# A third pair of decay buffers, in SBUF, for the Mamba stage of a four-layer cross-attention network

## The chip, the core and the metric

The kernel runs on one core of one Trainium2 chip. The metric is device time in microseconds (us) of that core. The kernel before takes 6634.21 us, the median of 3 runs (6632.14 to 6638.02).

## What is computed

Eight sequences x (512 x 256) and a short context of 64 x 192 for each pass through four blocks, all in float32: self-attention, cross-attention and feed-forward (L0), four Mamba layers on 64 + 512 positions (L1), cross-attention and feed-forward (L2), and a last cross-attention (L3). The change lies in L1, whose core is a scan over time for each of 512 channels and 16 states:

```
dt = softplus(einsum('bsr,er->bse', dt, dtp_w) + dtp_b)
A = -exp(A_log)
dA = exp(dt[..., None] * A)
dBu = dt[..., None] * Bm[:, :, None, :] * xi[..., None]
def step(h, t):
    da, dbu, c = t
    h = da * h + dbu
    return (h, einsum('bes,bs->be', h, c))
```

`dA` are the decays. The context is used by L0, by the 64 positions that go ahead of L1, and again by L2 and L3.

## The kernel before

The program is eight stages (`STAGES`). In the Mamba stage each of the 4 layers is cut into 9 chunks of `TC` = 512 positions, so there are 36 steps. In a step the 512 channels x 16 states are 64 units of 128 partitions x 512 positions, taken two at a time: 32 pairs, numbered j. Five engines run over the same 32 pairs, each in an order that is written out by hand, held together by semaphores.

- **ACT** (`@block.scalar`) makes the decays of a unit with an exponential (L2474) and writes them into PSUM, `banks[:, slot_of(i), :]`. There are two pairs of such buffers, PSUM banks 0, 1 and 2, 3, used in turn. Before it refills a pair it calls `slots_free` (L2123), which waits until the pair two before is done with it and copies the last column of that scan into `state` (L2129 or L2133), the start of the next step's scan. Between the pairs ACT does the rest of the layer: bias, Silu, Softplus, with loads of its function tables around them, at places given by `E_OUT`, `G_OUT`, `F_OUT`, `H_OUT`, `SILU_AT`.
- **POOL** (`@block.gpsimd`) writes dt * B * x of a pair into a ring of 6 pair buffers in SBUF (L2506), one instruction of 128 x 1024 on two SBUF tensors.
- **DVE** (`@block.vector`) scans each unit (L2429): inputs are the decays and the ring's entry. Of the 32 pairs, 22 are DVE's own: the scan writes over the decays in PSUM, and DVE then multiplies by C into the ring (`times_c`, L2237). The other 10 (`BY_POOL`) are POOL's: the scan writes into the ring, ACT copies the state and raises `kept`, and POOL multiplies by C (L2511). The multiplication of a pair's second half comes behind the next pair's first scan.
- **PE** (`@block.tensor`) sums each pair over the states (L2384), and `summed` gives the ring's place back to POOL. PE also does the layer's projections.
- **SP** (`@block.sync`) moves rows and weights by DMA.

All other tensors of the stage lie in `core.work` and `core.weights`, in SBUF. The PSUM has 8 banks: 0 to 3 hold decays, 4 and 5 sums, 6 and 7 the other results. `core.C` (128 x 2 x 512, SBUF) holds the context. The stage does not use it; `final_norm`, which comes next, reads it (L2558, L2688).

Of the kernel before, what the change touches and what calls it, by code (L numbers as in the profile page):

```python
# [18 lines left out]
ALU = mybir.AluOpType  # L19
ACT = mybir.ActivationFunctionType  # L20
AX = mybir.AxisListType

P = 128
B, T, D, DC = 8, 512, 256, 192
PRE, S1 = 64, 576
KD = D // P
M = 64
# [1704 lines left out]
TC = 512  # L1732
CHUNKS = B * S1 // TC
STEPS = LAYERS * CHUNKS
BODIES = 2 * CHUNKS
UN = 64
PAIRS_N = UN // 2
GROUPS = DI // 64
SP_ = DS // 2
BY_POOL = ((0, 5), (0, 3, 6), (0, 4), (0, 2, 4))  # L1740
NQ = sum(len(a) for a in BY_POOL)
ND = PAIRS_N - NQ
# [129 lines left out]
def val(N, per, off):  # L1872

    l, j = N
    return l * (BODIES * per) + (j * per + off)
# [31 lines left out]
    return BEFORE_S[name] if N[1] == -2 else val(N, len(LANE_S), S_BASE + LANE_S[name])  # L1907


def mamba(core):  # L1910
    at = 0
    ring, at = core.area(at, RING, 2, TC)
    dt_rep, at = core.area(at, 2, 2, TC)
# [7 lines left out]
    state, at = core.area(at, UN)  # L1921
    decay, at = core.area(at, UN)
# [5 lines left out]
    bc = core.weights[0][:, 0:SP_ * 2 * TC].rearrange("p (a c t) -> p a c t", a=SP_, c=2)  # L1928
# [22 lines left out]
    u_done, kept, saved = S("u_done"), S("kept"), S("saved")  # L1951
    rep_in = [S("rep_in0"), S("rep_in1")]
    da_full, fed, scanned, prod_d, prod_q, summed = S("da_full"), S("fed"), S("scanned"), S("prod_d"), S("prod_q"), S("summed")
    gated = S("gated")
    y_full, y_free, y_added = S("y_full"), S("y_free"), S("y_added")

    by_pool = lambda j: j % SP_ in BY_POOL[j // SP_]
    d_index = lambda j: sum(not by_pool(i) for i in range(j))
    q_index = lambda j: sum(by_pool(i) for i in range(j))
    slot_of = lambda i: 2 * (i // 2 % 2) + i % 2  # L1960
    da_full_at = lambda N, i: val(N, UN, i + 1)
    fed_at = lambda N, j: val(N, PAIRS_N, j + 2)
    scanned_at = lambda N, i: val(N, UN, i + 1)
    prod_d_at = lambda N, j: val(N, ND, d_index(j) + 3)
    saved_at = lambda N, j: val(N, ND, d_index(j) + 3)
    prod_q_at = lambda N, j: val(N, NQ, q_index(j) + 1)
    summed_at = lambda N, j: val(N, PAIRS_N, j + RING + 1)
    gated_at = lambda N, k: val(N, KI, k + 3)
# [151 lines left out]
        e.wait_ge(ln.v_full, v_at(N, f"H{tv}"))  # L2120
        e.activation(dt[:, tv, :], lane_v, ACT.Softplus, bias=lv("dt_b", tv)).then_inc(ln.v_free, 1)

    def slots_free(e, N, n, j):  # L2123

        M, j = (N, j - 2) if j >= 2 else (previous(N), PAIRS_N + j - 2)
        m = n if M[1] == N[1] else n - 1
        if N[1] >= 0 and by_pool(j):
            e.wait_ge(scanned, scanned_at(M, 2 * j + 1))
            e.activation(state[:, 2 * j:2 * j + 2], ring_pair(m, j)[:, :, TC - 1], ACT.Copy).then_inc(kept, 1)  # L2129
        elif N[1] >= 0:  # L2130
            s = slot_of(2 * j)
            e.wait_ge(prod_d, prod_d_at(M, j))
            e.activation(state[:, 2 * j:2 * j + 2], banks[:, s:s + 2, TC - 1], ACT.Copy).then_inc(saved, 1)  # L2133
            e.wait_ge(saved, saved_at(M, j))

    RESIDUAL = (19, 18)
# [97 lines left out]
    def times_c(e, N, n, j, h):  # L2234

        i = 2 * j + h
        last = e.tensor_tensor(ring_pair(n, j)[:, h, :], banks[:, slot_of(i), :], bc[:, j % SP_, 1, :], ALU.mult)  # L2237
        if h == 1:
            last.then_inc(prod_d, 1)

# [28 lines left out]
    def spread_u(e, k):  # L2269

        s = k % 2
        for h in range(2):
            for q in range(2):
                e.dma_start(u_rep[64 * q:64 * q + 64, s, h, :], u[64 * h:64 * h + 64, k, :]).then_inc(rep_in[s], 16)
# [6 lines left out]
    def load_bc(e, N, a, q, b):  # L2281

        e.dma_start(bc[64 * q:64 * q + 64, a, :, :], scratch[b][:, 2 * a + q, :].partition_broadcast(64)).then_inc(bc_ready[a // 2], 16)

    with core.nc.Block() as block:
        @block.sync
        def _(e):
            store_bc(e, (0, -1), 0)
            e.wait_ge(bc_stored, 16)
            for a in range(2):  # L2290
                for q in range(2):
                    load_bc(e, (0, -1), a, q, 0)
            e.wait_ge(u_done, u_done_at((0, -1), 0, 2))
            spread_dt(e, 0)
            spread_u(e, 0)
            for a in range(2, SP_):
                for q in range(2):
                    load_bc(e, (0, -1), a, q, 0)
            e.wait_ge(u_done, KI)
            for l in range(LAYERS // 2):  # L2300
                for j in range(BODIES):
                    N, c = (l, j), j % CHUNKS
                    layer = l * 2 + j // CHUNKS
                    after = (l * 2 + 2) % LAYERS if j >= CHUNKS else l * 2 + 1
                    e.wait_ge(summed, summed_at(previous(N), PAIRS_N - 1))
                    spread_dt(e, 1)
                    spread_u(e, 1)
                    if c == CHUNKS - 1:
                        load_z(e, core, after)
                    e.wait_ge(scanned, scanned_at(N, 15))  # L2310
                    spread_dt(e, 2)
                    spread_u(e, 2)
                    if c == CHUNKS - 2:
                        load_first(e, core, after)
                    store_bc(e, N, (j + 1) % 2)
                    e.wait_ge(scanned, scanned_at(N, 31))
                    spread_dt(e, 3)
                    e.wait_ge(bc_stored, val(N, 16, 32))
                    spread_u(e, 3)
                    if c == 0:  # L2320
                        load_out(e, core, layer)
                    e.wait_ge(u_done, u_done_at(N, 0, 2))
                    spread_u(e, 0)
                    e.wait_ge(scanned, scanned_at(N, 47))
                    spread_dt(e, 0)
                    if c == CHUNKS - 2:
                        load_middle(e, core, after)
                    for a in range(SP_):
                        pair = 3 * SP_ + a
                        if by_pool(pair):  # L2330
                            e.wait_ge(prod_q, prod_q_at(N, pair))
                        else:
                            e.wait_ge(prod_d, prod_d_at(N, pair))
                        load_bc(e, N, a, 0, (j + 1) % 2)
                        load_bc(e, N, a, 1, (j + 1) % 2)
            for a in range(SP_ // 2):
                e.wait_ge(bc_ready[a], 64 * (STEPS + 1))
            e.wait_ge(rep_in[0], 128 * (2 * STEPS + 1))
            e.wait_ge(rep_in[1], 128 * 2 * STEPS)
            e.wait_ge(core.first_loaded, FIRST_LOAD * (LAYERS + 1))  # L2340
            e.wait_ge(core.z_loaded, Z_LOAD * (LAYERS + 1))
            e.wait_ge(core.middle_loaded, MIDDLE_LOAD * (LAYERS + 1))
            e.wait_ge(core.out_loaded, OUT_LOAD * (LAYERS + 1))
# [50 lines left out]
        def _(e):  # L2394
# [15 lines left out]
            for l in range(LAYERS // 2):  # L2410
                for n in range(BODIES):
                    N, c = (l, n), n % CHUNKS
                    layer = l * 2 + n // CHUNKS
                    for i in range(UN):
                        j, h = i // 2, i % 2
                        k, a = j // SP_, j % SP_
                        if c == CHUNKS - 2 and i == SCALE_AT:
                            e.wait_ge(core.first_loaded, layer * FIRST_LOAD + 2 * FIRST_LOAD)
                        early_dve(e, N, i, c, normed[:, n % 2])
                        for f in range(KI - 1):  # L2420
                            if i == 16 * (f + 1) + 7:
                                gate(e, N, f, z[:, n % 2])
                        if i == 7:
                            gate(e, previous(N), KI - 1, z[:, (n + 1) % 2])
                        if h == 0:
                            e.wait_ge(fed, fed_at(N, j))
                        e.wait_ge(da_full, da_full_at(N, i))
                        da, ub = banks[:, slot_of(i), :], ring_pair(n, j)[:, h, :]
                        e.tensor_tensor_scan(ub if by_pool(j) else da, da, ub, state[:, i:i + 1], ALU.mult, ALU.add).then_inc(scanned, 1)  # L2429
                        if h == 0 and j > 0 and not by_pool(j - 1):  # L2430
                            e.wait_ge(scanned, scanned_at(N, i - 1))
                            times_c(e, N, n, j - 1, 1)
                        if h == 1 and not by_pool(j):
                            e.wait_ge(scanned, scanned_at(N, i - 1))
                            times_c(e, N, n, j, 0)
                        if h == 1 and j == PAIRS_N - 1 and not by_pool(j):
                            e.wait_ge(scanned, scanned_at(N, i))
                            times_c(e, N, n, j, 1)
# [8 lines left out]
        def _(e):  # L2447
# [9 lines left out]
            for l in range(LAYERS // 2):  # L2457
                for n in range(BODIES):
# [7 lines left out]
                    for i in range(UN):  # L2466
# [2 lines left out]
                        if i % 16 == 0:  # L2469
                            e.wait_ge(rep_in[k % 2], rep_at(N, k))  # L2470
                        if h == 0:
                            slots_free(e, N, n, j)
                        f = (2 * k + h) * SP_ + a
                        e.activation(banks[:, slot_of(i), :], dt_rep[:, k % 2, h, :], ACT.Exp, scale=decay[:, f:f + 1]).then_inc(da_full, 1)  # L2474
                        if c == CHUNKS - 1 and i == H_OUT[0]:
                            e.wait_ge(core.middle_loaded, layer * MIDDLE_LOAD + 2 * MIDDLE_LOAD)
                        if c == CHUNKS - 2 and i == E_OUT[0]:
# [351 lines left out]
```

## Time and profile before

| | before |
|---|---|
| median of 3 runs | 6634.21 us |
| the profiled execution, its time | 6639.8 us |
| the profiled execution, its span | 6638.0 us |
| Mamba stage, first scan to last | about 2054 to 5994 us, 3940 us |
| PE, DVE, POOL, ACT busy over the span | 92%, 74%, 66%, 55% |
| granted TensorE clock over the span | 0.941 of 2.4 GHz |

The profiled execution's time is its span and 1.8 us around it. A row of the lines view gives a line of the code, its engine and operation, what it writes and reads by name (`banks` is PSUM; `work`, `weights`, `C`, `X` are SBUF), the shape, the count, then busy time and mean length, and at the end how long the engine sat idle just before such instructions and for whom. A matmul's busy time has modelled ends, so PE's share is not to be taken for PE at its peak. An instruction's recorded length overlaps the next one's start a little on DVE and POOL.

### The profile page before, as it was taken

How to read it: one execution, taken by the hardware profiler on the slowest of the kernel's cores; microseconds unless marked ns; L12 is line 12 of the kernel's file. 1: busy time of each engine (PE TensorE's matmuls, PEld its weight loads, DVE VectorE, ACT ScalarE, POOL GpSimd, SP SyncE). 2: the span in 40 equal slices, each digit the busy share in tenths (PEclk: the TensorE clock that was granted, in tenths of full speed). 3: DMA queues.
4: the chain of work that ended last, by engine and by line, in shares of the span. 5: the costliest groups of instructions: out<-in, count | busy, mean ns of one | idle time of the engine just before them, and what ended most of it. 6: DMA issues, size and time to landing. Idle time of an engine off the chain costs nothing. (4 is left out here: it accounts for less than half of the span.)

```text
span 6638.0 us, 60681 instructions
## 1 busy us (share of the span) xinstructions
PE 6129.0 (92%) x20586; PEld 2577.4 (39%) x20586; DVE 4928.1 (74%) x5709; ACT 3620.5 (55%) x6605; POOL 4394.1 (66%) x2056
## 2 busy tenths in 40 slices
PE   9999999999999989898899989898989898988898
PEld 4555555544443333323333323333323343323444
DVE  4444445543225999999999999999999999995623
ACT  4444445432225666666666666666666666664432
POOL 3333334323005999999999999999999999992300
PEclk9999999999998989899989999999999898989998
DMA  2000000213002333333333333332333232332000
GB/s 80 1 1 1 1 1 1 86 26 102 20 0 68 83 76 78 78 93 85 72 89 71 83 88 86 71 89 65 89 81 93 65 89 65 93 80 56 4 0 26
DMA packets 228678, 387.64 MB, mean 58 GB/s; under 512 B 46304, under 2 KB 64416, under 8 KB 225936
## 3 DMA queue, kind: packets, MB, share of 16 engines
q1 hardware_dynamic: 228368, 383.75, 23.7%
q8 instruction: 164, 2.69, 0.2%
q14 instruction: 146, 1.20, 0.1%
HBM read 207.14 MB, written 23.40 MB: 35 GB/s over the span
## 5 line engine op out<-in xcount | busy, mean ns | idle before, releaser
L2506 POOL TENSOR_TENSOR work<-work,weights 128x1024 f32<-128x1024 f32 x1152 | 2685.6, 2361 | 15.8 <-PE banks L2384 6.8
L2429 DVE TENSOR_TENSOR_SCAN banks<-banks,work 128x512 f32<-128x512 f32 x1584 | 1985.7, 1272 | 53.5 <-ACT banks L2474 48.1
L2384 PE MATMUL banks<-work 128*64 128x512 f32 x4608 | 1353.9, 670 | 378.2 <-POOL work L2511 271.1
L2474 ACT ACTIVATE banks<-work 128x512 f32<-128x512 f32 x2304 | 1496.0, 680 | 25.5
L1992 PE MATMUL banks<-work,weights 128*128 128x512 f32 (+31 forms) x3796 | 1140.6, 451 | 3.0 <-DVE work L2222 3.0
L2237 DVE TENSOR_TENSOR work<-banks,weights 128x512 f32<-128x512 f32 x1584 | 1056.0, 668 | 0.0
L2511 POOL TENSOR_TENSOR work<-work,weights 128x1024 f32<-128x1024 f32 x360 | 848.0, 2356 | 238.4 <-ACT work L2129 238.4
L2429 DVE TENSOR_TENSOR_SCAN work<-banks,work 128x512 f32<-128x512 f32 x720 | 911.2, 1269 | 99.8 <-ACT banks L2474 97.2
L603 POOL TENSOR_TENSOR work<-work 128x1024 f32<-128x1024 f32 x256 | 479.6, 1893 | 743.4 <-DVE work L470 742.9
L1992 PEld LDWEIGHTS banks<-work,weights 128*128 128x128 f32 x3796 | 634.4, 190 | 600.0 <-issue 523.6
L2133 ACT ACTIVATE work<-banks 128x2 f32<-128x2 f32 x792 | 135.9, 172 | 1227.4 <-DVE work L2237 1225.6
L2384 PEld LDWEIGHTS banks<-work 128*64 128x64 f32 x4608 | 271.0, 145 | 1236.4 <-issue 500.8
L553 ACT ACTIVATE work<-banks,work 128x512 f32<-128x512 f32 x512 | 347.7, 690 | 201.1 <-DVE work L464 201.1
L464 DVE TENSOR_REDUCE work<-banks 128x2 f32<-128x1024 f32 x256 | 308.8, 1214 | 105.1 <-PE banks L389 104.7
L2010 PE MATMUL banks<-work,weights 128*128 128x512 f32 x592 | 350.7, 722 | 0.0
L1040 PE MATMUL banks<-work,weights 128*128 128x512 f32 x768 | 341.5, 599 | 9.4 <-ACT work L215 9.4
L454 DVE COPY work<-banks 128x512 f32<-128x512 f32 x256 | 175.5, 685 | 160.3 <-PE banks L379 160.3
L379 PE MATMUL banks<-ident,work 128*128 128x128 f32 x2048 | 277.9, 279 | 8.2 <-DVE work L454 4.6
L379 PEld LDWEIGHTS banks<-ident,work 128*128 128x128 f32 x2048 | 222.1, 141 | 151.7 <-issue 111.1
L389 PE MATMUL banks<-work 64*128 64x512 f32 x1024 | 254.4, 615 | 0.0
L366 PE MATMUL banks<-work 128*64 128x256 f32 x2048 | 247.5, 385 | 0.0
L322 PE MATMUL banks<-work,weights 128*128 128x512 f32 x512 | 224.9, 597 | 6.4 <-ACT work L215 4.2
(312 smaller groups left out, 6796.9 us busy)
## 6 DMA issues: line engine op xcount, KB each, us to landing
weights<-mamba_bc SPq DMA_DIRECT2D x592, 256.0 KB, 5.0
work<-work SPq DMA_DIRECT2D x1160, 128.0 KB, 2.3
weights<-mamba_taps SPq DMA_DIRECT2D x5, 2048.0 KB, 7.5
weights<-cross_vo SPq DMA_DIRECT2D x16, 512.0 KB, 6.9
mamba_taps<-work SPq DMA_DIRECT2D x4, 2048.0 KB, 7.8
cross_vo<-weights SPq DMA_DIRECT2D x6, 1024.0 KB, 8.4
work<-in_conv_rows SPq DMA_DIRECT2D x16, 256.0 KB, 6.7
out_T<-X SPq DMA_DIRECT2D x8, 512.0 KB, 3.3
```

Source lines behind the costliest of these rows:

```text
L379: mm = e.transpose(core.banks[:, 4 + j, kt * P:(kt + 1) * P], probs[:, 2 * (g % 2) + u, j, kt * P:(kt + 1) * P], core.ident[:])
L553: last = e.activation(probs[:, slot, j, :], core.banks[:, 2 * u + j, :], ACT.Exp, bias=nmax[:, slot, j:j + 1], accum_out=sums[:, slot, j:j ...
L603: e.tensor_tensor(probs[:, slot], probs[:, slot], rsum[:, slot, :].unsqueeze(2).to_broadcast([P, 2, T]), ALU.mult) \
L1040: mm = e.matmul(bank(i), w1[:, k, m * P:(m + 1) * P], normed[:, k, :], start=(k == 0), stop=(k == KD - 1))
L1992: mm = e.matmul(lane[:, a:b], conv_w[j][:, k, m * P:(m + 1) * P], nb[:, k, a + j:b + j], start=(d == 0 and k == 0), stop=(j == 0 and b == ...
L2010: mm = e.matmul(lane, z_w[:, k, m * P:(m + 1) * P], nb[:, k, TAPS - 1:], start=(k == 0), stop=(k == KD - 1))
L2237: last = e.tensor_tensor(ring_pair(n, j)[:, h, :], banks[:, slot_of(i), :], bc[:, j % SP_, 1, :], ALU.mult)
L2384: mm = e.matmul(ybank[k % 2][64 * h:64 * h + 64, :], fold, ring_pair(n, j)[:, h, :], start=False, stop=(a == SP_ - 1))
L2429: e.tensor_tensor_scan(ub if by_pool(j) else da, da, ub, state[:, i:i + 1], ALU.mult, ALU.add).then_inc(scanned, 1)
L2474: e.activation(banks[:, slot_of(i), :], dt_rep[:, k % 2, h, :], ACT.Exp, scale=decay[:, f:f + 1]).then_inc(da_full, 1)
L2506: e.tensor_tensor(ring_pair(n, j), u_rep[:, k % 2], bc[:, a, 0, :].unsqueeze(1).to_broadcast([P, 2, TC]), ALU.mult) \
L2511: e.tensor_tensor(ring_pair(n, q), ring_pair(n, q), bc[:, q % SP_, 1, :].unsqueeze(1).to_broadcast([P, 2, TC]), ALU.mult) \
```

## The change

The decays get a third pair of buffers: `core.C`, the context's place. `decay_slots` gives each of the 36 x 32 pairs the buffer that was used longest ago. In the last step only the two PSUM pairs are used, and SP loads the context back into `core.C` from DRAM there (`reload_context`). `slots_free` now waits for the pair that had the same buffer, mostly three before, and copies the states of all pairs up to it. In `saved_at` (L1965) the offset 3 becomes 1, since the copies are now counted from the first pair on.

```diff
+def decay_slots():
+    slot, earlier, last = [], [], [None, None, None]
+    for g in range(STEPS * PAIRS_N):
+        slots = range(3) if g < (STEPS - 1) * PAIRS_N else range(2)
+        s = min(slots, key=lambda t: -1 if last[t] is None else last[t])
+        slot.append(s)
+        earlier.append(last[s])
+        last[s] = g
+    return slot, earlier
...
-    slot_of = lambda i: 2 * (i // 2 % 2) + i % 2
+    slot, earlier = decay_slots()
+    decays = [banks[:, 0:2, :], banks[:, 2:4, :], core.C[:]]
+    pair_at = lambda N, j: val(N, PAIRS_N, j)
+    decay_pair = lambda N, j: decays[slot[pair_at(N, j)]]
...
-    def slots_free(e, N, n, j):
-        M, j = (N, j - 2) if j >= 2 else (previous(N), PAIRS_N + j - 2)
...
+    def keep_state(e, g):
+        M, j = step_of(g), g % PAIRS_N
+        if by_pool(j):
             e.wait_ge(scanned, scanned_at(M, 2 * j + 1))
+            e.activation(state[:, 2 * j:2 * j + 2], ring_pair(M[1], j)[:, :, TC - 1], ACT.Copy).then_inc(kept, 1)
+        else:
             e.wait_ge(prod_d, prod_d_at(M, j))
+            e.activation(state[:, 2 * j:2 * j + 2], decay_pair(M, j)[:, :, TC - 1], ACT.Copy).then_inc(saved, 1)
+
+    def slots_free(e, N, j):
+        g = earlier[pair_at(N, j)]
+        if g is None:
+            return
+        before = earlier[pair_at(N, j) - 1]
+        for m in range(0 if before is None else before + 1, g + 1):
+            keep_state(e, m)
...
-        last = e.tensor_tensor(ring_pair(n, j)[:, h, :], banks[:, slot_of(i), :], bc[:, j % SP_, 1, :], ALU.mult)
+        last = e.tensor_tensor(ring_pair(n, j)[:, h, :], decay_pair(N, j)[:, h, :], bc[:, j % SP_, 1, :], ALU.mult)
...
+    def reload_context(e):
+        M, j = step_of(last_in_c), last_in_c % PAIRS_N
+        e.wait_ge(saved, saved_at(M, j)) if not by_pool(j) else e.wait_ge(scanned, scanned_at(M, 2 * j + 1))
+        e.dma_start(core.C[:, 0, :], core.dram["ctxT"][0:P]).then_inc(context_back, 16)
+        for r in (0, DC - P):
+            e.dma_start(core.C[r:r + DC - P, 1, :], core.dram["ctxT"][P:DC]).then_inc(context_back, 16)
...
-                        da, ub = banks[:, slot_of(i), :], ring_pair(n, j)[:, h, :]
+                        da, ub = decay_pair(N, j)[:, h, :], ring_pair(n, j)[:, h, :]
```

On DVE, this is a stretch in the middle of the stage. L2429 of before and L2466 of after are the scan (shown by its class of instruction, SCALAR_TENSOR_TENSOR), L2237 and L2263 the multiplication by C. Before:

```order
L2429 SCALAR_TENSOR_TENSOR banks<-banks,work 128x512 x2
L2237 TENSOR_TENSOR work<-banks,weights 128x512
L2429 SCALAR_TENSOR_TENSOR banks<-banks,work 128x512
L2237 TENSOR_TENSOR work<-banks,weights 128x512
L2429 SCALAR_TENSOR_TENSOR banks<-banks,work 128x512
L2237 TENSOR_TENSOR work<-banks,weights 128x512
L2429 SCALAR_TENSOR_TENSOR banks<-banks,work 128x512
L2237 TENSOR_TENSOR work<-banks,weights 128x512
```

The same stretch after:

```order
L2466 SCALAR_TENSOR_TENSOR banks<-banks,work 128x512 x2
L2263 TENSOR_TENSOR work<-banks,weights 128x512
L2466 SCALAR_TENSOR_TENSOR C<-C,work 128x512
L2263 TENSOR_TENSOR work<-banks,weights 128x512
L2466 SCALAR_TENSOR_TENSOR C<-C,work 128x512
L2263 TENSOR_TENSOR work<-C,weights 128x512
L2466 SCALAR_TENSOR_TENSOR banks<-banks,work 128x512
L2263 TENSOR_TENSOR work<-C,weights 128x512
```

The order on DVE is the same. What differs is where the decays of every third pair lie: two scans and, in a pair of DVE's own, two multiplications read C in the place of banks.

On ACT, this is the stretch ahead of a Softplus (L2185 and L2211 load its table; L2133 and L2148 copy a state, L2129 and L2145 one of POOL's pairs, L2474 and L2511 make decays). Before:

```order
L2129 ACTIVATE work<-work 128x2
L2474 ACTIVATE banks<-work 128x512 x2
L2190 ACTIVATE work<-banks 128x512
L2133 ACTIVATE work<-banks 128x2
L2474 ACTIVATE banks<-work 128x512 x2
L2129 ACTIVATE work<-work 128x2
L2474 ACTIVATE banks<-work 128x512 x2
L2185 ACT_TABLE_LOAD
```

After:

```order
L2145 ACTIVATE work<-work 128x2
L2511 ACTIVATE banks<-work 128x512 x2
L2148 ACTIVATE work<-C 128x2
L2511 ACTIVATE C<-work 128x512 x2
L2211 ACT_TABLE_LOAD
```

The number of decays is the same. Each is asked for one pair earlier against the state that is copied ahead of it, and every third pair goes to C.

## Rows read from the trace of the kernel before

**Rows 1.** The page: the span and the busy time by engine.

```profile
span 6638.0 us, 60681 instructions
PE 6129.0 (92%) x20586; PEld 2577.4 (39%) x20586; DVE 4928.1 (74%) x5709; ACT 3620.5 (55%) x6605; POOL 4394.1 (66%) x2056
```

**Rows 2.** Busy time in stretches: the Mamba stage, then one sparse stretch of PE.

```profile
core 0: us, PE busy (x) PEld busy (x) DVE busy (x) ACT busy (x) POOL busy (x), PEclk, DMA share, GB/s
2054.00:5994.00 3940.00, 3561.79 (x10573) 1301.16 (x10571) 3808.31 (x4103) 2535.20 (x4505) 3684.90 (x1662) 0.92 0.35 81
...
2240.00:2250.00 10.00, 7.17 (x12) 1.67 (x12) 9.94 (x11) 8.09 (x13) 8.83 (x5) 0.54 0.00 0
```

**Rows 3.** Waits of DVE in the stage: in total us, times, longest.

```profile
DVE work L2429 <- ACT banks L2474: 97.2, 37, 25.8
DVE banks L2429 <- ACT banks L2474: 48.1, 41, 6.4
```

**Rows 4.** Timeline, DVE, 3066 to 3076 us: start, length.

```profile
3068.58 0.67 DVE L2237 TENSOR_TENSOR work<-banks,weights 128x512 f32<-128x512 f32 x1
3069.17 1.28 DVE L2429 TENSOR_TENSOR_SCAN banks<-banks,work 128x512 f32<-128x512 f32 x1
3070.36 0.67 DVE L2237 TENSOR_TENSOR work<-banks,weights 128x512 f32<-128x512 f32 x1
3073.42 1.28 DVE L2429 TENSOR_TENSOR_SCAN work<-banks,work 128x512 f32<-128x512 f32 x1 [2.39 <-ACT banks L2474]
```

**Rows 5.** Timeline, ACT, the same stretch.

```profile
3067.90 1.28 ACT L2173 ACT_TABLE_LOAD   x1
3069.20 1.91 ACT L2173 ACTIVATE work<-work 128x2048 f32<-128x2048 f32 x1
3071.13 1.28 ACT L2174 ACT_TABLE_LOAD   x1
3072.42 0.17 ACT L2133 ACTIVATE work<-banks 128x2 f32<-128x2 f32 x1
3072.63 1.30 ACT L2474 ACTIVATE banks<-work 128x512 f32<-128x512 f32 x2
```

**Rows 6.** By line: count, length min/median/max, of DVE's and POOL's instructions in the stage.

```profile
L2237 DVE TENSOR_TENSOR work<-banks,weights x1584: 656/669/678, 2065.3 to 5994.5; 128x512 f32<-128x512 f32 x198
...
L2506 POOL TENSOR_TENSOR work<-work,weights x1152: 2332/2358/2426, 2047.8 to 5985.2; 128x1024 f32<-128x1024 f32 x192
```

**Rows 7.** By line: the same, outside the stage, both inputs in SBUF.

```profile
L1678 DVE TENSOR_TENSOR work<-work x4: 691/986/994, 6569.7 to 6625.6; 128x512 f32<-128x512 f32 x4
...
L1588 POOL TENSOR_TENSOR work<-work x8: 1266/1272/1726, 6558.6 to 6607.4; 128x512 f32<-128x512 f32 x8
...
L191 DVE SCALAR_TENSOR_TENSOR work<-work,vec x34: 741/746/1745, 15.9 to 6512.6; 128x512 f32<-128x512 f32 x34
...
L1812 POOL TENSOR_TENSOR work<-work x12: 1260/1264/1708, 1617.8 to 1666.2; 128x512 f32<-128x512 f32 x12
```

**Rows 8.** Timeline, 6568 to 6572 us, last attention.

```profile
6568.86 2.95 POOL L1588 TENSOR_TENSOR work<-work 128x512 f32<-128x512 f32 x2 [7.31 <-ACT work L1703]
6569.69 0.99 DVE L1678 TENSOR_TENSOR work<-work 128x512 f32<-128x512 f32 x1
```

**Rows 9.** Timeline, 1619 to 1623 us, feed-forward.

```profile
1617.79 4.15 POOL L1812 TENSOR_TENSOR work<-work 128x512 f32<-128x512 f32 x3
...
1620.03 2.46 DVE L191 SCALAR_TENSOR_TENSOR work<-work,vec 128x512 f32<-128x512 f32 x2 [3.40 <-ACT work L208]
```

**Rows 10.** Timeline, POOL, from 3052 us: four feeds in a row.

```profile
3052.30 9.36 POOL L2506 TENSOR_TENSOR work<-work,weights 128x1024 f32<-128x1024 f32 x4
```

**Rows 11.** DMA issues, the first load of the context: KB each, us to landing.

```profile
C<-in_ctxT SPq DMA_DIRECT2D x1, 256.0 KB, 11.7
C<-in_ctxT SPq DMA_DIRECT2D x2, 128.0 KB, 10.3
```

More of the change, by code:

```diff
@@ L1953, in mamba @@
     da_full, fed, scanned, prod_d, prod_q, summed = S("da_full"), S("fed"), S("scanned"), S("prod_d"), S("prod_q"), S("summed")
-    gated = S("gated")
+    gated, context_back = S("gated"), S("context_back")
     y_full, y_free, y_added = S("y_full"), S("y_free"), S("y_added")
@@ L1959, in mamba @@
     q_index = lambda j: sum(by_pool(i) for i in range(j))
-    slot_of = lambda i: 2 * (i // 2 % 2) + i % 2
+    slot, earlier = decay_slots()
+    decays = [banks[:, 0:2, :], banks[:, 2:4, :], core.C[:]]
+    pair_at = lambda N, j: val(N, PAIRS_N, j)
+    decay_pair = lambda N, j: decays[slot[pair_at(N, j)]]
+    step_of = lambda g: (0, g // PAIRS_N)
+    last_in_c = max(g for g in range(STEPS * PAIRS_N) if slot[g] == 2)
     da_full_at = lambda N, i: val(N, UN, i + 1)
@@ L1964, in mamba @@
     prod_d_at = lambda N, j: val(N, ND, d_index(j) + 3)
-    saved_at = lambda N, j: val(N, ND, d_index(j) + 3)
+    saved_at = lambda N, j: val(N, ND, d_index(j) + 1)
     prod_q_at = lambda N, j: val(N, NQ, q_index(j) + 1)
@@ L2121, in soft_plus @@
         e.activation(dt[:, tv, :], lane_v, ACT.Softplus, bias=lv("dt_b", tv)).then_inc(ln.v_free, 1)
-    def slots_free(e, N, n, j):
-        M, j = (N, j - 2) if j >= 2 else (previous(N), PAIRS_N + j - 2)
-        m = n if M[1] == N[1] else n - 1
-        if N[1] >= 0 and by_pool(j):
+    def keep_state(e, g):
+        M, j = step_of(g), g % PAIRS_N
+        if by_pool(j):
             e.wait_ge(scanned, scanned_at(M, 2 * j + 1))
-            e.activation(state[:, 2 * j:2 * j + 2], ring_pair(m, j)[:, :, TC - 1], ACT.Copy).then_inc(kept, 1)
-        elif N[1] >= 0:
-            s = slot_of(2 * j)
+            e.activation(state[:, 2 * j:2 * j + 2], ring_pair(M[1], j)[:, :, TC - 1], ACT.Copy).then_inc(kept, 1)
+        else:
             e.wait_ge(prod_d, prod_d_at(M, j))
-            e.activation(state[:, 2 * j:2 * j + 2], banks[:, s:s + 2, TC - 1], ACT.Copy).then_inc(saved, 1)
+            e.activation(state[:, 2 * j:2 * j + 2], decay_pair(M, j)[:, :, TC - 1], ACT.Copy).then_inc(saved, 1)
[6 more added lines that the diff above has]
+            keep_state(e, m)
+        M, j = step_of(g), g % PAIRS_N
+        if not by_pool(j):
             e.wait_ge(saved, saved_at(M, j))
@@ L2307, in _ @@
                     spread_u(e, 1)
+                    if pair_at(N, 0) == (STEPS - 1) * PAIRS_N:
+                        reload_context(e)
                     if c == CHUNKS - 1:
@@ L2339, in _ @@
             e.wait_ge(rep_in[1], 128 * 2 * STEPS)
+            e.wait_ge(context_back, 48)
             e.wait_ge(core.first_loaded, FIRST_LOAD * (LAYERS + 1))
@@ L2471, in _ @@
                         if h == 0:
-                            slots_free(e, N, n, j)
+                            slots_free(e, N, j)
                         f = (2 * k + h) * SP_ + a
-                        e.activation(banks[:, slot_of(i), :], dt_rep[:, k % 2, h, :], ACT.Exp, scale=decay[:, f:f + 1]).then_inc(da_full, 1)
+                        e.activation(decay_pair(N, j)[:, h, :], dt_rep[:, k % 2, h, :], ACT.Exp, scale=decay[:, f:f + 1]).then_inc(da_full, 1)
                         if c == CHUNKS - 1 and i == H_OUT[0]:
```

## The prediction

> **What bounds the kernel now.** I read the page first, then busy time by stretch, then waits, then timelines. The page [rows 1] shows no engine full over the span: PE 92% by its modelled ends, DVE 74%, POOL 66%. The stretch of the Mamba stage [rows 2] is another picture: in its 3940 us DVE is busy 3808 (97%), POOL 3685 (94%), PE 3562 and ACT 2535 (64%). So DVE sets the pace there, and POOL is close behind. The waits of DVE [rows 3] name what is left: 97.2 + 48.1 = 145.3 us in 78 waits, all for the decays from ACT. One of them is 25.8 us, the fill ahead of the first scan. That leaves 119.5 us, 3.3 us in each of the 36 steps.
>
> The timelines show how such a wait comes about. DVE ends a multiplication, and its next scan starts only at 3073.42, 2.39 us late [rows 4]. Before that, ACT had loaded a table (1.28 us), done a Silu (1.91 us) and loaded the first table back (1.28 us), and only then made the decays [rows 5]: 4.5 us away from its main work. With two pairs of buffers ACT can be at most that far ahead that such an absence shows.
>
> **The change, part by part.** The sum is made against the profiled execution's 6639.8 us, 5.6 us above the median of the runs.
>
> *ACT's lead.* A third pair of buffers lets ACT be one pair further ahead. A pair of DVE's takes two scans and two multiplications: start to start 1.19 us for a scan and 0.59 for a multiplication [rows 4], 3.56 us together. The waits to be covered are 119.5 / 77 = 1.6 us on average, so I take them all as gone: **-120 us**. Bounds: 0 if something else holds ACT, -120 if nothing does. ACT's copies and exponentials stay the same in number, and it has 36% to spare.
>
> *Where the decays lie.* `decay_slots` can be counted: from step 0 to 34 every third pair goes to C, 373 of them, of which 255 are DVE's own and 118 POOL's; the last step has none. So 746 scans and 510 multiplications now have both inputs in SBUF (C and the ring, C and `bc`), where all of them had one in PSUM. This is what decides. The stage has no such instruction on DVE now, and its rows are calm although DVE and POOL overlap nearly all the time: 669 ns, at most 678, for a multiplication, and at most 2426 for a feed of POOL [rows 6]. But there are such instructions outside of it, and those with two SBUF inputs that meet a POOL instruction are not calm [rows 7]: L1678 takes 691 ns at least and 986 in the middle, one L191 takes 1745 where the median is 746, and POOL's own L1588 and L1812 go from 1272 to 1726 and from 1264 to 1708.
>
> The timelines say what happens. In [rows 8] POOL starts two instructions at 6568.86; the first would end by 6570.13. DVE starts at 6569.69, in the middle of it, takes 0.99, which is 0.30 over 0.69, so it worked only from 6569.99, and ended at 6570.68. POOL's second took 0.45 too long, that is, until 6570.54. **They took turns**: DVE waited for POOL's instruction to end (less 0.14 us that can overlap), then POOL waited for DVE's. In [rows 9] two L191 stand back to back: 2.46 us for the two, where 1.41 would do. The first slipped in at the end of a POOL instruction; then POOL's next got its turn, and the second L191 waited a full 1.745 - 0.746 = 1.00 us for POOL's 1.26. So behind a DVE instruction with two SBUF inputs that made POOL queue, a second one waits for a whole POOL instruction less 0.26 us.
>
> This case's rows agree with a rule of the Trainium skill, "SBUF — State Buffer", section "Who interferes with whom": a DVE instruction with two SBUF inputs contends with a GpSimd instruction that reads SBUF, as an exclusive lock for the whole instruction, and one with at most one SBUF input does not. By that rule the change turns a gain into a large loss; without it, the sum would be the first rival below.
>
> *DVE's waits.* A POOL instruction here is 2.36 us long (2.33 start to start, from 9.36 for four [rows 10]). A turn behind it costs at most 2.36 - 0.26 = 2.10 us, less what DVE does in between that needs no turn. Were POOL always busy, a C pair of DVE's own would pay: first scan, at any point of POOL's instruction, 2.36 / 2 - 0.16 = 1.02; second scan, with one free multiplication (0.59) in between, 1.51; first multiplication, right behind it, 2.10; second one, behind a free scan (1.19), 0.91; together 5.54 us. Behind one of POOL's pairs (118 of the 255) there is no multiplication in between, 0.59 more. A C pair of POOL's pays 1.02 + 1.51 = 2.53. In all 255 x 5.54 + 118 x 0.59 + 118 x 2.53 = 1413 + 70 + 299 = 1782 us.
>
> POOL isn't always busy. It has 3685 us of work [rows 2]. A multiplication holds it up for 0.45 us, a scan, which is 0.60 longer, for 1.05 (no row has a scan with two SBUF inputs; the bounds are nothing, and its full 1.27): 746 x 1.05 + 510 x 0.45 = 1013 us. If the stage becomes 5340 us, POOL is at work in 3685 / (5340 - 1013) = 0.85 of the time in which it could be. So 0.85 x 1782 = **+1515 us**, and 3940 + 1515 - 120 = 5335 fits what I put in. With 691 ns in the place of 669 [rows 6, 7], 510 multiplications cost **+11 us**.
>
> *The rest.* The reload of the context is three DMAs that landed in 10 to 12 us when they were issued first [rows 11]. It is issued once the last C pair's state is copied, in the first pairs of the last step, and the stage's end is some 100 us behind it: nothing. Were it late, it would cost these 12 us once. The three issues stand ahead of `spread_dt(2)`, which waits for half a step anyway. ACT writing C in the place of PSUM: ACT isn't the bound, nothing. `kept` comes from ACT in the same order relative to the scan.
>
> Sum: 6639.8 - 120 + 1515 + 11 = 8046, so **8040 us**.
>
> **The rivals.**
>
> 1. *No turns for this pattern* (the other side). If the scan and this multiplication could read both inputs from SBUF beside POOL, only the two small terms are left: 6639.8 - 120 + 11 = 6531 us, faster. It speaks for it that no row shows a scan with two SBUF inputs, and it decides at the first C scan that overlaps POOL. Against it: three L1678 and one L191, different operations, all took their turn. Price of being wrong: the whole 1515. Chance 0.04.
>
> 2. *The change gives ACT no lead*, because it waits for something else (PE's results, which it would now want a pair sooner), and there are no turns: 6639.8 + 11, within the measurement. Chance 0.02.
>
> 3. *Only the multiplication takes turns.* 255 pairs x (1.02 + 0.91) x 0.88 = 433, so 6639.8 - 120 + 11 + 433 = 6964 us. The same holes in the rows speak for it. Chance 0.05.
>
> 4. *POOL becomes the bound, and DVE's waits fall into its gaps.* POOL's gaps are when it waits for a scan of its own pairs, so the two might lock in step. The floor is POOL's work and what holds it up, 3685 + 1013 = 4698 us for the stage, 758 over 3940: 7398 us. Chance 0.17.
>
> 5. *POOL is always in the way, or PE joins in.* At a full 1782 us the time is 6639.8 - 120 + 11 + 1782 = 8313 us. PE could help: in a stretch in which it is busy 7.2 of 10 us its granted clock is 0.54, against 0.92 over the stage [rows 2], so it runs between its two levels of 1.2 and 2.4 GHz, and a PE with more gaps has more of the lower. Its work is 3562 x 0.92 = 3277 us at the full clock; at a mean of 0.6 this is 5462 us, 130 more than my stage, 8170 us. Chance 0.10.
>
> My forecast has 0.62.
>
> **How the numbers follow.** The prediction is the likeliest, 8040. The range goes from 7300, just under POOL's floor, to 8350, just over a full set of waits. Outside are rivals 1 to 3 (0.11) and some 0.06 for tails. About 0.2% (13 us) is what a measurement of this kernel can tell from no change: faster by more 0.04, within 0.02, slower by more 0.94 (rivals 3, 4, 5 and the forecast).
>
> **What would show it.** In the profile after, the scan that writes C should be long on average, with a wide spread: 1.27 plus some 1.1 to 1.3 us of turns, while those on banks stay at 1.27. The multiplication from C should stand at 0.69 plus some 1.3. The recorded idle of DVE should be near nothing, since these waits lie inside the instructions; waits for ACT should be gone. POOL's L2506 should go from a maximum of 2.43 to well over 3 us, and sum to about 1000 us more. Other stages stay as they are. If the C scan's mean is 1.27 the mechanism is wrong; if it is long but POOL is idle less than a tenth of the stage, it is rival 4; if PE's clock falls below 0.7 and DVE waits for PE, it is rival 5.

## The result and the profile after

The changed kernel takes 7948.11 us (median of 4 runs, 7943.99 to 7955.24) against 6635.4 for the kernel before: a ratio of 1.198, 95% interval 1.196 to 1.200. The forecast was 8040, its range 7300 to 8350. The profiled execution has a span of 7942.2 us, 1304.2 more than before.

First the stage in one stretch (busy time of PE, PEld, DVE, ACT, POOL, then PE's granted clock), against [rows 2]:

```profile
2054.00:7303.00 5249.00, 3930.55 (x10580) 1379.14 (x10579) 5197.38 (x4104) 2564.82 (x4504) 4328.42 (x1662) 0.83 0.25 61
```

The Mamba stage grew from 3940 to 5249 us, which is all of the difference (5 us more than it, since this stretch ends 2.3 us behind the start of the stage's last multiplication and that of [rows 2] just before it, and since the rest of the kernel got 2 us shorter). DVE's busy time grew by 1389 us for the same work, and its idle time fell from 132 to 52. Which instructions grew is in the lines view, in the page of the profile after (count, busy time, mean, idle before):

```profile
L2543 POOL TENSOR_TENSOR work<-work,weights 128x1024 f32<-128x1024 f32 x1152 | 3197.9, 2802 | 64.8 <-PE banks L2421 59.1
...
L2466 DVE TENSOR_TENSOR_SCAN banks<-banks,work 128x512 f32<-128x512 f32 x1074 | 1344.0, 1269 | 20.5 <-ACT banks L2511 13.1
...
L2466 DVE TENSOR_TENSOR_SCAN C<-C,work 128x512 f32<-128x512 f32 x510 | 1131.2, 2234 | 27.7 <-ACT C L2511 22.7
...
L2263 DVE TENSOR_TENSOR work<-C,weights 128x512 f32<-128x512 f32 x510 | 980.8, 1925 | 0.0
...
L2263 DVE TENSOR_TENSOR work<-banks,weights 128x512 f32<-128x512 f32 x1074 | 711.2, 664 | 0.0
...
L2466 DVE TENSOR_TENSOR_SCAN work<-C,work 128x512 f32<-128x512 f32 x236 | 557.0, 2364 | 0.0
```

Instructions that read `banks` kept their 1.27 and 0.66 us. Those that read C pay 0.96 us more (scans of DVE's own pairs), 1.09 (scans of POOL's pairs) and 1.26 (multiplications): 510 x 0.96 + 236 x 1.09 + 510 x 1.26, with unrounded means 1391 us. The spread, by line (min/median/max), says that they wait and don't work more slowly:

```profile
L2466 DVE TENSOR_TENSOR_SCAN C<-C,work x510: 1248/2240/3441, 2065.7 to 7182.4; 128x512 f32<-128x512 f32 x170
...
L2263 DVE TENSOR_TENSOR work<-C,weights x510: 655/1642/2833, 2070.1 to 7188.9; 128x512 f32<-128x512 f32 x170
```

The fastest need what one on `banks` needs (the multiplication 655 ns), and the slowest 2.2 us more, which is nearly one POOL product (2.36). A single turn can be followed in the timelines of DVE and of POOL:

```profile
3010.79 5.23 DVE L2466 TENSOR_TENSOR_SCAN C<-C,work 128x512 f32<-128x512 f32 x2
```

```profile
3009.36 5.57 POOL L2543 TENSOR_TENSOR work<-work,weights 128x1024 f32<-128x1024 f32 x2
```

DVE asks at 3010.79, POOL's first product runs until about 3011.7. DVE scans for its 1.2 us, POOL's second product then has its 2.3 us until 3014.93, and only then DVE does the second scan, until 3016.02. Alone the pair would take 2.44 us. This is the pattern of [rows 8, 9]. It holds throughout: taken one by one, 319 instructions on C start inside a POOL product of the stage that was not itself held up, and all of them wait, until 2.15 to 2.28 us after the product's start.

### The profile page after: what moved, and what is told of

Same layout as the page of the kernel before. It is cut to its first block and busy times, and to the rows that moved or that the text cites. A ratio compares the mean times of both kernels' runs of the same rounds, so it can differ in the third digit from the quotient of the medians.

```text
span 7942.2 us, 60682 instructions
## 1 busy us (share of the span) xinstructions
PE 6494.4 (82%) x20586; PEld 2651.3 (33%) x20586; DVE 6317.8 (80%) x5709; ACT 3651.1 (46%) x6603; POOL 5037.8 (63%) x2056
## 5 line engine op out<-in xcount | busy, mean ns | idle before, releaser
L2543 POOL TENSOR_TENSOR work<-work,weights 128x1024 f32<-128x1024 f32 x1152 | 3197.9, 2802 | 64.8 <-PE banks L2421 59.1
L2548 POOL TENSOR_TENSOR work<-work,weights 128x1024 f32<-128x1024 f32 x360 | 929.6, 2582 | 852.8 <-ACT work L2145 852.8
L2466 DVE TENSOR_TENSOR_SCAN banks<-banks,work 128x512 f32<-128x512 f32 x1074 | 1344.0, 1269 | 20.5 <-ACT banks L2511 13.1
L2466 DVE TENSOR_TENSOR_SCAN C<-C,work 128x512 f32<-128x512 f32 x510 | 1131.2, 2234 | 27.7 <-ACT C L2511 22.7
L2511 ACT ACTIVATE banks<-work 128x512 f32<-128x512 f32 x1558 | 1011.0, 679 | 17.7
L2263 DVE TENSOR_TENSOR work<-C,weights 128x512 f32<-128x512 f32 x510 | 980.8, 1925 | 0.0
L2263 DVE TENSOR_TENSOR work<-banks,weights 128x512 f32<-128x512 f32 x1074 | 711.2, 664 | 0.0
L2466 DVE TENSOR_TENSOR_SCAN work<-banks,work 128x512 f32<-128x512 f32 x484 | 611.4, 1267 | 27.0 <-ACT banks L2511 26.8
L2466 DVE TENSOR_TENSOR_SCAN work<-C,work 128x512 f32<-128x512 f32 x236 | 557.0, 2364 | 0.0
L2148 ACT ACTIVATE work<-C 128x2 f32<-128x2 f32 x255 | 51.6, 202 | 1040.4 <-DVE work L2263 1040.4
L2511 ACT ACTIVATE C<-work 128x512 f32<-128x512 f32 x746 | 497.2, 712 | 8.4
L2148 ACT ACTIVATE work<-banks 128x2 f32<-128x2 f32 x535 | 89.9, 168 | 799.2 <-DVE work L2263 799.0
L2027 PE MATMUL banks<-work,weights 128*128 128x512 f32 x592 | 371.5, 760 | 0.0
L1040 PE MATMUL banks<-work,weights 128*128 128x512 f32 x768 | 342.6, 600 | 9.8 <-ACT work L215 9.8
```

Source lines behind the costliest of these rows:

```text
L1040: mm = e.matmul(bank(i), w1[:, k, m * P:(m + 1) * P], normed[:, k, :], start=(k == 0), stop=(k == KD - 1))
L2027: mm = e.matmul(lane, z_w[:, k, m * P:(m + 1) * P], nb[:, k, TAPS - 1:], start=(k == 0), stop=(k == KD - 1))
L2263: last = e.tensor_tensor(ring_pair(n, j)[:, h, :], decay_pair(N, j)[:, h, :], bc[:, j % SP_, 1, :], ALU.mult)
L2511: e.activation(decay_pair(N, j)[:, h, :], dt_rep[:, k % 2, h, :], ACT.Exp, scale=decay[:, f:f + 1]).then_inc(da_full, 1)
L2543: e.tensor_tensor(ring_pair(n, j), u_rep[:, k % 2], bc[:, a, 0, :].unsqueeze(1).to_broadcast([P, 2, TC]), ALU.mult) \
L2548: e.tensor_tensor(ring_pair(n, q), ring_pair(n, q), bc[:, q % SP_, 1, :].unsqueeze(1).to_broadcast([P, 2, TC]), ALU.mult) \
```

## Experiments

Turns are the waits of DVE and POOL for each other that the prediction describes. The kernel before took 6639.9 us beside e1 to e4, 6639.0 beside e5 to e8 and 6642.4 beside e9 to e12. e3, e4 and e9 to e12 were executed once each, the others 4 to 11 times. DVE's waits for ACT are given without the one ahead of the stage's first scan, some 25 us in every run (in e1 that one is put down to POOL).

**e1 and e2: POOL reads nothing.** Both kernels with POOL's two products of the stage replaced by fills with zero, so the products are left out of the result. Edit, in each (the operands are shortened):

```diff
-e.tensor_tensor(ring_pair(n, j), u_rep[:, k % 2], bc[...], ALU.mult).then_inc(fed, 1)
+e.memset(ring_pair(n, j), 0.0).then_inc(fed, 1)
-e.tensor_tensor(ring_pair(n, q), ring_pair(n, q), bc[...], ALU.mult).then_inc(prod_q, 1)
+e.memset(ring_pair(n, q), 0.0).then_inc(prod_q, 1)
```

> The kernel before, with POOL's two products of the Mamba stage (feed and product with C) replaced by fills with zero of the same 128 x 1024: POOL still writes the ring and keeps all waits, but reads nothing (the two products are left out of the result). It is the partner of the next run. Turns theory: nothing to take turns with before either, DVE stays at 1.27 and 0.67 us and waits some 120 us for ACT: about 6630 us (6600 to 6640). Rival (POOL's reads slow DVE or ACT in general): clearly below 6600.

> The changed kernel, decays of every third pair in C as before, with POOL's two products of the Mamba stage replaced by fills with zero (left out of the result). Turns theory (DVE with two SBUF inputs against a POOL instruction that reads SBUF): with POOL reading nothing, the scans on C fall to 1.27 us and the products from C to 0.67, DVE's waits for ACT shrink from 120 to about 40, and the time is 6520 to 6560 us, below its partner. Rival (C is slow by itself, two SBUF inputs against ACT, PE or DMA traffic): the scans stay at 2.2 to 2.4 us and the time near 7900. Second rival (POOL's writes collide as well): in between, about 7000.

e1: 6622.8 us, e2: 6754.8 us. The turns theory holds on the instructions, in the source view of e2:

```profile
L2466 DVE TENSOR_TENSOR_SCAN C<-C,work x510: 1248/1269/3254, 2068.3 to 5999.7; 128x512 f32<-128x512 f32 x170
...
L2263 DVE TENSOR_TENSOR work<-C,weights x510: 655/668/2794, 2071.3 to 6002.6; 128x512 f32<-128x512 f32 x170
```

C in SBUF isn't slow by itself, POOL's writes don't collide, and the time is 1193 us below the changed kernel's. A few stay long. The trace puts them beside POOL's dt * x (L2278), which still reads SBUF: of the 51 instructions on C that are over 0.15 us too long, 48 wait while it runs (78 us in all), and the other 3 beside a small product of POOL's (2 us). e1 came out as expected, but e2 misses its forecast: it is 132 us *above* its partner, not 80 below. Of this, 79 us are DVE's busy time (these last turns). The rest is waits for ACT, which grew from 100 to 160 us. The third pair gave ACT no lead even without turns. Why is in ACT's waits, in the kernel before and then in e2 (L2178, L2187 and L2169 are L2152, L2161 and L2143 of before; the other two had no wait there):

```profile
ACT work L2152 <- PE banks L2010: 39.9, 36, 6.9
...
ACT work L2161 <- PE banks L1992: 29.1, 35, 2.3
ACT X L2143 <- PE banks L2043: 16.2, 36, 0.5
```

```profile
ACT work L2187 <- PE banks L2009: 156.3, 36, 6.1
ACT work L2178 <- PE banks L2027: 147.6, 36, 7.8
ACT work L2222 <- PE banks L2027: 146.9, 35, 4.9
ACT work L2219 <- PE banks L2027: 136.8, 35, 4.2
ACT X L2169 <- PE banks L2060: 124.5, 36, 3.6
```

ACT takes PE's results at fixed places, mostly three pairs behind the place where PE makes them (four or five for a few). With a lead of three pairs it gets there first, and waits up to 4 to 8 us in its order, with the next decays queued behind. In total it waits 828 us for PE, against 123 before and 75 in e1. That this order is the cause is tested next.

**e5 and e6: the same two, ACT's other work one pair later.** Edit (of `E_OUT` the last place, and of `H_OUT` the last, by one unit only, since SP's loads rely on them):

```diff
-    E_OUT, G_OUT, F_OUT, SILU_AT = (59, 3, 9, 13), 29, (55, 49, 33, 1), (15, 7)
-    H_OUT = (37, 45)
+    E_OUT, G_OUT, F_OUT, SILU_AT = (61, 5, 11, 14), 31, (57, 51, 35, 3), (17, 9)
+    H_OUT = (39, 46)
-    RESIDUAL = (19, 18)
+    RESIDUAL = (21, 20)
-    SQUARE_AT, RSTD_AT, SCALE_AT = 5, (21, 23), 26
+    SQUARE_AT, RSTD_AT, SCALE_AT = 7, (23, 25), 26
```

> Run e2 (third pair in C, POOL only fills) with ACT's other work of a step placed one pair (two units) later, two places of it one unit later. In e2 ACT came to these places a pair sooner than PE had the results and waited 822 us for PE, against 75 us in e1, so the third pair gave it no lead. Order theory: one pair later undoes this, ACT's waits for PE fall to 100 to 300 us, DVE's waits for ACT from 186 to about 60 us, and the time from 6755 to 6620 to 6650 us (some 77 us of turns with POOL's remaining reads stay in). Rival (ACT can't use a lead, something else holds it): no change, 6740 to 6770 us.

> Run e1 (two pairs, POOL only fills) with the same places one pair later, as the control of e5. Order theory: with two pairs ACT waited only 75 us for PE at these places, so little is to be had, and the work only moves: 6610 to 6650 us. If the later places alone were worth it, this run would gain over 50 us from 6623 as well.

e5: 6592.5 us, 162 below e2. e6: 6726.0 us, 103 *above* e1. ACT's wait for PE is 112 us in e5 and 10 in e6; DVE's waits for ACT fell to 22 us in e5 and rose to some 220 in e6. Both times lie outside what was expected (6620 to 6650, and 6610 to 6650), each further in its own direction. So the order theory holds, and more sharply than I expected: the places fit the lead on both sides. For two pairs the late places delay what PE needs back: in e6 the weight loads of L2107 wait 108 us and its matmuls 46 for banks that ACT has yet to read, and not at all in e1. How this comes back to DVE was not followed further. For three pairs the late places are right. A third pair is worth 30 us here (e5 against e1) with turns nearly absent, and only with the order changed with it.

**e3 and e4: who may use C.** Only POOL's pairs, or only DVE's own (`pool` says whether the pair is one of POOL's):

```diff
-        slots = range(3) if g < (STEPS - 1) * PAIRS_N else range(2)
+        slots = range(3) if g < (STEPS - 1) * PAIRS_N and pool else range(2)
```

(e4: `not pool`; in both, and in e9, `slots_free` copies from the latest pair copied so far.)

> The changed kernel, but only pairs of POOL's may take the third pair of buffers: 279 of them do, so 558 scans have two SBUF inputs, and no multiplication of DVE's. Turns theory: each scan pays what it paid in the changed kernel, 1.09 us, 608 us in all, less 0 to 80 for ACT's lead: 7160 to 7250 us. Rival 3 of the prediction (only the multiplication takes turns): 6560 to 6640 us.

> The changed kernel, but only pairs of DVE's own may take the third pair of buffers: 315 of them do, so 630 scans and 630 multiplications have two SBUF inputs. Turns theory at the prices of the changed kernel (0.96 us a scan, 1.26 a multiplication): 605 + 794 = 1399 us, less up to 80 for ACT's lead: 7950 to 8040 us. If POOL were the bound (rival 4) the time would go by what holds POOL up instead, 630 x 1.05 + 630 x 0.45 = 945 over 3685, against 1013 there: 60 to 70 us below the changed kernel, about 7880.

e3: 7305.9 us.

```profile
L2468 DVE TENSOR_TENSOR_SCAN work<-C,work 128x512 f32<-128x512 f32 x558 | 1358.7, 2440 | 38.2 <-POOL work L2545 38.2
```

This settles rival 3: with no multiplication from C, 558 scans average 2.440 us, 1.17 over 1.27, which is 653 of the 666 us over the kernel before. A scan takes turns as a multiplication does. The time is 56 us above the upper end of what I expected. A turn of these scans cost 1.17 us and not 1.09, which is 45 us, and the lead gave nothing in sum: the waits for ACT fell from 119.5 to 82 us, and those for POOL rose from 3 to 65. e4: 7752.9 us, below both numbers expected. The scans pay 0.77 and the multiplications 1.06, 1153 us together, less than in the changed kernel. So the price of a turn isn't fixed. A wait ends with POOL's instruction, so what it costs goes by how much of that instruction is left; why DVE came at better moments here was not looked into.

**e9: the place without the lead.** `slots = (0, 2)` in the place of `range(3)`, and `(0, 1)` in the last step.

> No third pair: the two pairs of decay buffers are one in PSUM and one in C (the other PSUM pair is used in the last step only). ACT's lead is that of the kernel before, so this is the place alone: 560 pairs in C, 490 of DVE's own and 70 of POOL's, 1120 scans and 980 multiplications with two SBUF inputs. Turns theory at the prices of the changed kernel (own pair 2 x 0.96 + 2 x 1.26 = 4.44 us, POOL's 2.19): 2176 + 153 = 2329 us more at an unchanged share of POOL; POOL's share of the time falls as the stage grows, so some 15% less: 8600 to 8950 us. Rival 4 (POOL the bound): what holds POOL up is 1120 x 1.05 + 980 x 0.45 = 1617, stage 5302, time about 8000.

8565.8 us, just under the range, and far from the 8000 of rival 4.

```profile
L2466 DVE TENSOR_TENSOR_SCAN C<-C,work 128x512 f32<-128x512 f32 x980 | 1983.7, 2045 | 7.5 <-ACT C L2511 6.5 <-issue 1.0
L2263 DVE TENSOR_TENSOR work<-C,weights 128x512 f32<-128x512 f32 x980 | 1886.3, 1928 | 0.0
```

980 scans at 2.045, 140 at 1.635 and 980 multiplications at 1.928 us pay 760 + 51 + 1235 = 2046 us. The time grew by 1923, since nearly all waits for ACT are gone. The loss comes with the place, not with the third pair, and grows with the number of C pairs.

**e11: shorter turns.** POOL's products of 128 x 1024 as two of 128 x 512 (the feed is shown; the product with C is split alike):

```diff
-e.tensor_tensor(ring_pair(n, j), u_rep[:, k % 2], bc[...], ALU.mult).then_inc(fed, 1)
+for h in range(2):
+    done = e.tensor_tensor(ring_pair(n, j)[:, h, :], u_rep[:, k % 2, h, :], bc[:, a, 0, :], ALU.mult)
+done.then_inc(fed, 1)
```

> The changed kernel, each of POOL's 128 x 1024 products as two of 128 x 512 (same result). Turns theory: a turn now costs DVE at most 1.26 - 0.26 = 1.00 us in the place of 2.10: scans on C pay about 0.4 us (1.0 before), multiplications from C 0.5 (1.3 before), 560 us in all, and the longest C scan is about 2.3 us, not 3.4. POOL's own work grows by 1512 x 0.2 = 300 us, and with what DVE holds up it gets near the bound: 7250 to 7600 us. Rival (both slow down by sharing, not by whole turns): the C scan's mean stays at 2.2 to 2.4 us and the time near 8000.

7765.3 us. The multiplication fell from 1.925 to 1.221 us, less than half of its excess, as expected. The scan fell only from 2.234 to 1.945 (1.67 expected). Its longest is still 3.3 us, since I had forgotten that dt * x stays whole: beside that one the turns reach this length, and beside the halves no instruction on C is over 2.41 us. But only 57 us of turns are beside dt * x, so why the scan's mean stayed high is open. DVE's turns fell from 1391 to 788 us, but its waits rose from 75 to 460, with the first one in both: 256 us for POOL, which is now slow in feeding, and 204 for ACT. The direction holds; the size of the scan's turn and the total (7250 to 7600 expected) don't. The rival, in which both engines slow down by sharing, has the scan's mean unchanged and is out.

**e10: POOL with one SBUF input.** The products replaced by `e.tensor_scalar(..., 0.5, None, ALU.mult)`, so both are left out of the result.

> The changed kernel, with POOL's two products of the Mamba stage replaced by one SBUF input times a constant (the product with B and with C is left out of the result). Turns theory, any POOL instruction that reads SBUF: scans on C and multiplications from C are longer than 1.27 and 0.67 in about the share of time in which POOL is busy, by up to POOL's instruction less 0.26 us; with POOL's instruction near 1 us, some 0.2 to 0.5 us each, 6900 to 7200 us. Rival (only POOL instructions with two inputs collide): as e2, 6755 us, C scans at 1.27 in the median.

```profile
L2466 DVE TENSOR_TENSOR_SCAN C<-C,work x510: 1251/1274/3318, 2065.0 to 6785.9; 128x512 f32<-128x512 f32 x170
...
L2543 POOL TENSOR_SCALAR work<-work x1152: 2758/2766/3775, 2046.3 to 6904.7; 128x1024 f32<-128x1024 f32 x192
```

7561.7 us, and neither theory is right as it stood. This form takes POOL 2.77 us, longer than the product of two inputs (2.36), so POOL bounds the stage and DVE waits 456 us for it. The scans on C stand at 1.27 in the median while POOL is busy nearly all the time, but the means are 1.473 and 1.527 (multiplication 1.011): most meet no turn, some do. Which ones do can be read from DVE's timeline beside POOL's:

```profile
3002.92 3.22 DVE L2466 TENSOR_TENSOR_SCAN work<-C,work 128x512 f32<-128x512 f32 x2 [3.00 <-POOL work L2543]
...
3023.47 2.44 DVE L2466 TENSOR_TENSOR_SCAN C<-C,work 128x512 f32<-128x512 f32 x2
```

```profile
3000.12 11.32 POOL L2543 TENSOR_SCALAR work<-work 128x1024 f32<-128x1024 f32 x4
...
3014.14 14.32 POOL L2543 TENSOR_SCALAR work<-work 128x1024 f32<-128x1024 f32 x5
```

The second instruction of POOL's four starts at 3002.85. A scan comes 0.07 us later and takes 2.05 us, 0.78 too long. The scan behind it starts 2.04 us into the same instruction and isn't delayed. Nor is the one at 3023.47, which starts 1.13 us into an instruction of POOL's. Taken one by one, 859 instructions on C start inside one of these that was not itself held up. The 281 that start in its first 0.65 us wait, until about 0.84 us after its start; the 578 that start from 0.78 us on don't wait at all, though POOL works for 2 us more. So here a turn behind POOL lasts 0.84 us of its 2.77, where beside a product of two inputs it lasted 2.15 of 2.36. What POOL does in the rest of the time no run shows.

**e12: the changed kernel with ACT's later places**, the edit of e5 with POOL's products whole.

> The changed kernel, POOL's products whole, with ACT's other work one pair later as in e5. DVE's waits for ACT are only 37 us there, but ACT's waits for PE 701. Order theory: those 37 us go, ACT copies POOL's pairs a little sooner, 7890 to 7940 us. The order can't be worth the 162 us of e5 here, since turns, not ACT, set DVE's pace: if it is, my account of the 1304 us is wrong.

7941.1 us, 7 below, which is less than the changed kernel's own runs differ (11 us), and 1 above what was expected. DVE's waits for ACT are some 9 us and those for POOL are gone, and the turns grew by as much (1430 us in the place of 1391). The order isn't worth here what it is in e5, and DVE's pace is set by turns.

**e7 and e8: a version for the kernel before.** Two pairs in PSUM; ACT refills each half of a pair as soon as that half is free, and in e8 all of ACT's other places are one unit later:

```diff
-            e.wait_ge(prod_d, prod_d_at(M, j))
-            e.activation(state[:, 2 * j:2 * j + 2], banks[:, s:s + 2, TC - 1], ACT.Copy).then_inc(saved, 1)
+            e.wait_ge(prod_h if h == 0 else prod_d, prod_d_at(M, j))
+            e.activation(state[:, 2 * j + h:2 * j + h + 1], banks[:, s, TC - 1:TC], ACT.Copy).then_inc(saved, 1)
...
-        if h == 1:
-            last.then_inc(prod_d, 1)
+        last.then_inc(prod_h if h == 0 else prod_d, 1)
```

> The kernel before (two pairs in PSUM, POOL unchanged), but ACT refills each of a pair's two buffers as soon as that half is free: a semaphore counts DVE's first multiplication too, and behind one of POOL's pairs the first half is free after its own scan. One small copy of ACT's more per pair. ACT's lead grows by up to half a pair, 1.8 us, with no decay in SBUF, so no turns. Theory (the lead counts as long as PE is not yet waited for): DVE's waits for ACT fall from 119 to about 60 us, time 6570 to 6600 us. Rival (ACT then waits for PE): 6625 to 6650 us.

> Run e7 with ACT's other work of a step one unit (half a pair) later, which goes with the half pair of lead. Order theory: waits of ACT for PE fall below those of e7 and DVE's waits for ACT with them: 6550 to 6590 us, not above e7. Rival (no lead is lost to PE in e7): equal to e7 within 10 us.

e7: 6642.1 us, ratio 1.0004 (0.9996 to 1.0013): no gain, as the rival had it. DVE's waits for ACT stayed (118 us), and the lead went into ACT's waits for PE, 233 us against 123. e8: 6598.4 us, ratio 0.994 (0.993 to 0.995), 8 us above what was expected. **It is faster than both kernels, by 40 us against the kernel before**, with DVE's waits in the stage:

```profile
DVE work L2432 <- ACT banks L2476: 73.1, 37, 25.4
DVE banks L2432 <- ACT banks L2476: 34.0, 68, 5.2
```

That is 82 us without the first 25.4, against 119.5 [rows 3]. What the places one unit later would do without the half release was not run.

## Why the prediction was right, and where not

- **What decides** was right: both inputs in SBUF make DVE and POOL take turns. The rows outside the stage [rows 7 to 9] carried over to the scan, for which there was no row; e2 and e3 show it.
- **DVE's waits.** Forecast 0.85 x 1782 = 1515 us, measured 1391. One term of it was clearly mis-sized, how long DVE holds POOL up. I had 1.05 us for a scan and 0.45 for a multiplication, each time, 1013 us; POOL's busy time grew by 4328 - 3685 = 643. Often POOL was between two products, waiting for `kept`, whose waits grew from 238 to 853 us. With 643 in the same formula and the measured stage, the share is 3685 / (5249 - 643) = 0.80 and the waits 1426 us.
- **That sum comes close, but the parts don't.** A smaller share would lower every kind of turn alike. By kind, the forecast's own terms give 0.85 x 255 x (2.10 + 0.91) = 652 us for the multiplications, and they measured 641; 254 for the scans of POOL's pairs, measured 258; and 0.85 x (255 x (1.02 + 1.51) + 70) = 608 for DVE's own scans, measured 492. So nearly all of the 124 us lies in the own scans: 0.96 us each and not 1.19, below the 1.1 to 1.3 that the prediction had as its sign. Why these came at better moments is open. The prices also move between runs with the same POOL products: in e12 a multiplication paid 1.44 us and not 1.26.
- **ACT's lead, -120 us.** This step failed as it was reasoned, though two thirds of its size appeared: DVE's waits for ACT fell by 82 us (119.5 to 37.3) while the stage grew by 1309. e2 shows that without turns the third pair takes nothing away (100 us in e1, 160 in e2), since ACT then waits for PE. That was the condition of rival 2, to which I gave 0.02; its mechanism was real, and turns covered it. So that the term came out with the right sign was luck. "If nothing does" needed a look at how far behind PE ACT's fixed places are: mostly three pairs.
- **+11 us** for longer instructions was nothing: 655 ns is the least from C and 653 from PSUM. Why L1678 takes 691 at the least is open.
- **The reload and the rest** cost nothing visible: from the start of the last multiplication by C to the end it is 641.5 us (7942.2 - 7300.7), against 643.5 before.
- The sum: -82 for waits for ACT, +1391 for turns, +10 for waits for POOL, +1319; the span grew by 1304. Rivals 1, 3 and 4 are ruled out by the long C scans, by e3, and by POOL's idle share (18% of the stage, where rival 4 had under a tenth). Of rival 5, PE's clock fell from 0.92 to 0.83 in the stage, and DVE's waits for PE in the stage did not grow (4 us before, none after).

## What to carry to other kernels

Before a buffer moves from PSUM to SBUF, count the SBUF inputs of the DVE instructions that read it, and look for a stretched instruction of that kind elsewhere in the trace: compared with its own median it shows what a turn with POOL costs. A deeper buffer gives an engine a lead only if its other fixed work moves with it, as in e5 and e8.

## What was not expected of the hardware

On POOL a 128 x 1024 float32 product of one SBUF input with a constant took 2.77 us, longer than that of two SBUF inputs (2.36), and it delayed DVE's two-input instructions only if they started in its first 0.65 us, until 0.84 us after its start (e10). A fill of the same size took 0.95 us, and DVE's scans beside it were not delayed (e2, median 1.269 us). ACT wrote decays to C in 707 ns in the median, to PSUM in 673.

The Trainium skill, "SBUF — State Buffer", section "Who interferes with whom", says that a DVE instruction with two SBUF inputs contends with a GpSimd one that reads SBUF and not with one that only writes. The runs agree on two inputs (e3) and on the fill (e2). On one input e10 agrees only for the first 0.84 us of 2.77, and there the measurement decides.
